# Where the resident slots are prepared at two changes of the resident set: one subtraction at the end of each quarter's list instead of up to two

## What is computed

```python
def ref(hidden_states, cross_attention_states, ...):   # 32 query heads, 8 key/value heads, width 128
    q = rmsnorm(hidden_states @ q_proj_w.T)            # per head
    k = rmsnorm(cross_attention_states @ k_proj_w.T)
    v = cross_attention_states @ v_proj_w.T
    attn = softmax(q @ k.T * scale + mask)
    return (attn @ v) @ o_proj_w.T

x = x + tanh(g_xattn) * ref(layernorm(x), ctx, ...)
x = x + tanh(g_ffn) * experts(layernorm(x), A, B, Wr)  # top 16 of 64 experts of rank 16, softmax gates
```

## Time and profile before

| | us |
|---|---|
| median of three runs | 2317.74 (2317.13 to 2318.9) |
| the profiled execution | 2318.4 |
| its span, first to last instruction | 2316.6 |
| TensorE busy | 2261.6 (98%) |
| VectorE busy | 1597.6 (69%) |
| ScalarE busy | 1183.9 (51%) |
| GpSimd busy | 1144.8 (49%) |
| mean granted clock of TensorE | 0.997 of full speed |

### The profile page before, as it was taken

How to read it: one execution, slowest core, us unless ns; L and a number is a source line. 1 busy time by engine, 2 the same in 40 slices (tenths; PEclk the granted TensorE clock), 3 DMA queues, 4 the chain that set the end, 5 groups by cost and what they waited for, 6 DMA issues and landing times.

```text
span 2316.6 us, 35630 instructions
## 1 busy us (share of the span) xinstructions
PE 2261.6 (98%) x11615; PEld 1906.0 (82%) x11615; DVE 1597.6 (69%) x2669; ACT 1183.9 (51%) x3773; POOL 1144.8 (49%) x1735
## 2 busy tenths in 40 slices
PE   6999999999999999999999999999999999999999
PEld 5887887888888878888888788888888887888787
DVE  7558558777777797777777954755756878555755
ACT  5546546666666676666666732422424335333421
POOL 3666566666555555555555453233232664534221
PEclk9999999999999999999999999999999999999999
DMA  5688466767667367764322635645557566323643
GB/s 198 218 245 296 150 197 232 212 165 204 183 170 191 121 212 205 230 179 128 110 91 92 209 100 164 182 127 166 162 152 216 186 217 255 128 92 136 237 164 136
DMA packets 177062, 408.78 MB, mean 176 GB/s; under 512 B 11824, under 2 KB 77616, under 8 KB 159664
## 3 DMA queue, kind: packets, MB, share of 16 engines
q1 hardware_dynamic: 169392, 351.97, 44.1%
q0 software_dynamic: 7488, 54.53, 12.9%
HBM read 282.72 MB, written 190.84 MB: 204 GB/s over the span
## 4 chain that ended last, share of the span: by engine, by line
PE 84%; DVE 4%; POOL 4%; issue 3%; ACT 3%; DMA 2%; SPq 0%; POOLq 0%; ACTq 0%; DVEq 0%
PE bank L769 23%; PE bank L771 23%; PE bank L770 23%; PE bank L827 4%; PE bank L835 2%; PE bank L815 2%; DVE t_lo L1320 1%; PE bank L852 1%; PE bank L851 1%; PE bank L850 1%; ACT t_hi L1024 1%; POOL s_hi L1811 1%; DVE s_lo L1320 1%; DMA t_raw<-combos 1%; DMA staged<-in_w_q 1%
## 5 line engine op out<-in xcount | busy, mean ns | idle before, releaser
L769 PE MATMUL bank<-t_hi,s_hi 128*128 128x512 f32 x2688 | 1084.0, 403 | 30.7 <-DVE t_lo L1320 17.3
L771 PE MATMUL bank<-t_hi,s_lo 128*128 128x512 f32 x2688 | 1053.8, 392 | 0.0
L770 PE MATMUL bank<-t_lo,s_hi 128*128 128x512 f32 x2688 | 1050.9, 391 | 0.0
L769 PEld LDWEIGHTS bank<-t_hi,s_hi 128*128 128x128 f32 x2688 | 507.2, 189 | 128.1 <-issue 32.3
L771 PEld LDWEIGHTS bank<-t_hi,s_lo 128*128 128x128 f32 x2688 | 505.8, 188 | 110.7
L1320 DVE TENSOR_TENSOR s_lo<-staged,s_hi 128x512 fp32r<-128x512 f32 x672 | 525.0, 826 | 88.9 <-ACT s_hi L1035 86.9
L770 PEld LDWEIGHTS bank<-t_lo,s_hi 128*128 128x128 f32 x2688 | 507.5, 189 | 90.3
L1035 ACT CAST s_hi<-staged 128x512 fp32r<-128x512 f32 x434 | 250.2, 623 | 184.9 <-POOL staged L1801 71.5
L1782 POOL TENSOR_SCALAR small<-small 128x4 f32<-128x4 f32 (+1 forms) x192 | 75.9, 395 | 446.9 <-ACT small L1131 341.4
L1799 POOL TENSOR_TENSOR staged<-staged 128x512 f32<-128x512 f32 x86 | 115.3, 1340 | 365.5 <-DMA staged<-heads 196.9
L1463 DVE SCALAR_TENSOR_TENSOR probs<-bank,small,mask 128x128 f32<-128x128 f32 x512 | 143.9, 343 | 87.1 <-POOL small L1789 43.6
(11 more groups left out here) (143 smaller groups left out, 2894.7 us busy)
## 6 DMA issues: line engine op xcount, KB each, us to landing
heads<-heads SPq DMA_DIRECT2D x128, 256.0 KB, 4.3
staged<-in_w_q SPq DMA_DIRECT2D x32, 768.0 KB, 5.2
staged<-heads SPq DMA_DIRECT2D x32, 768.0 KB, 6.9
sums<-sums POOLq DMA_DIRECT2D x24, 1024.0 KB, 8.0
t_raw<-in_sets SPq DMA_DIRECT2D x20, 1024.0 KB, 7.1
t_raw<-combos SPq DMA_DIRECT2D x19, 1024.0 KB, 8.6
xt<-x_columns SPq DMA_DIRECT2D x8, 1792.0 KB, 6.8
combos<-in_sets POOLq DMA_DIRECT2D x14, 1024.0 KB, 10.2
```

Source lines behind the costliest of these rows:

```text
L769: nc.tensor.matmul(out, s_hi[w][:, cols], high, start=start, stop=False, skip_group_check=True)
L770: nc.tensor.matmul(out, s_hi[w][:, cols], low, start=False, stop=False, skip_group_check=True)
L771: done = nc.tensor.matmul(out, s_lo[w][:, cols], high, start=False, stop=at == 3, skip_group_check=True)
```

## The change

It adds a third table of positions and uses it at the changes to sets 3 and 4 only.

```diff
+FILL_POSITIONS_QUERY = (2, 4, 6, 7, 9, 11, 11)
...
-            positions = FILL_POSITIONS_AHEAD if t in AHEAD_SETS else FILL_POSITIONS
+            positions = FILL_POSITIONS_QUERY if t in (3, 4) else FILL_POSITIONS_AHEAD if t in AHEAD_SETS else FILL_POSITIONS
```

## The result

| | before | changed |
|---|---|---|
| median of 7 runs, us | 2318.17 (2317.13 to 2319.04) | 2325.74 (2322.92 to 2327.12) |
| profiled execution, span | 2318.4, 2316.6 | 2324.77, 2323.0 |

The change makes the kernel slower: the ratio is 1.003 with a 95% interval of 1.0021 to 1.004, 7.6 us between the medians. The prediction said 2324.6, 6.9 above before.

The account below looks back on a forecast made before the run. TensorE, busy 98% of the span, was taken as the bound, with VectorE late at set changes. Waits of +4.1 and clock drops of +2.8 gave +6.9 us, 2324.6 on the median; range 2318.5 to 2329.5.

Parts of the forecast that it names:

- What bounds: At the two set changes VectorE is the late engine and TensorE waits; 6.7 and 6.8 us lost, 13.5 the prize.
- The first quarters give back: First two quarters of the new set shorten as VectorE's lists start earlier; 3.8 us in hand by the third.
- Slot 4: Third quarter of the new set: subtraction starts at 851.27, giving TensorE a new wait of 3.0 us.
- Slot 5: Third quarter's seventh part: subtraction usable at 861.0 to 861.8, a second new wait of 2.5 to 3.3, taken as 2.9.
- The clock: Half-clock drops behind the waits for slots 4 and 5: +1.4 us a change, +2.8 in all, bounds 0 and 6.6.
- the term for the waits alone: TensorE's waits at both set changes together, without any clock drop: +4.1 us.
- Totals: Both set changes: +4.1 us of waits and +2.8 of clock, +6.9 us in all.
- Rival 1: No clock drop at the set changes, the waits alone: +4.1 or +3.3, 2321 to 2322 us; chance 0.17.
- Rival 2: Two full clock drops at each set change, neither hidden: +10.7 us, 2328.4; chance 0.15.
- Rival 4: No difference: VectorE's lists run about 1 us shorter each change and the clock stays, within 3 us; chance 0.07.
- Rival 3: Faster: VectorE regains its ordinary distance before slot 4 is due, 7.6 us faster, 2310.1; chance 0.06.
- The rule on the oscillating clock: Skill's rule that waits make following work begin at half clock; all four long waits paid twice, +10.7 us.

Follow-up runs that it names:

- e6: Changed kernel with the four sums of staged formed for only 16 of 512 columns at the changes to sets 3 and 4: 2325.72 us, ratio 1.0032.
- e8: Kernel before with the four sums of staged formed for only 16 of 512 columns at the changes to sets 3 and 4: 2313.89 us, ratio 0.998.
- e2: Changed kernel with slots 4 and 5 each put back by one quarter: 2318.21 us, ratio 0.9995 to before.
- e3: Kernel before with slot 2 alone moved one quarter later, beside slot 3: 2318.91 us, ratio 1.0004.
- e9: Changed kernel with slot 4's and 5's subtractions ahead of the softmax in the same quarters, their ScalarE copies earlier: 2317.22 us, ratio 0.9996 to before.
- e5: Changed kernel with spare matmuls on TensorE, 10 ahead of slot 4's part and 8 ahead of slot 5's: 2324.19 us, ratio 1.0024 to before.
- e4: Kernel before with slots 5 and 6 alone moved to the third quarter of the new set's first quad: 2325.15 us, ratio 1.0025.
- e7: Changed kernel with slot 4's subtraction moved to GpSimd and slots 5 and 6 put back to the new set's second quarter: 2324.13 us, ratio 1.0027 to before.

## Why the prediction was right

**What bounds.** Right. The loss lies in the two stretches and the quarter behind each, and VectorE is full up to new r2 in nearly every version; in e6, with less work, it waits. e8 bears it out from the other side: with less VectorE work the kernel before gains 4.6 us, while none of the three other orders of the same work gained anything (e2, e3, e9 within their intervals). e8 also has `staged` ready earlier, and no run separates the two.

**The first quarters give back.** Right, and a little too small. Predicted starts of new r1 and r2, counted from new r0, were 8.15 and 17.55; they came at 7.92 and 16.90. The wait before L836 in new r0 was 0.40 and not 0.8, the one before L828 0.20 and not 0.8, and the second one before L836 1.01 against 1.25. The wait for s_lo went as said.

**Slot 4.** Right: subtraction predicted at 851.27, measured at 850.68; wait predicted at 3.0, measured at 2.77 and 3.01.

**Slot 5.** Right in place and cause: VectorE's own wait of 0.5 is there (0.55), the subtraction started at 858.95 (predicted 858.6 to 859.4) and was usable at 861.8 (861.0 to 861.8). The waits are 3.69 and 1.81 where I took 2.9 for both, with bounds of 2.5 and 3.3 that neither keeps. In the first change TensorE was at full clock and at the part earlier than I had it (858.12 against 858.47), and the subtraction lasted 2.76. In the second the clock had dropped behind slot 4, so that TensorE reached the part later: the half clock was hidden in this wait, as the section on the clock supposed. Slot 6 caused no wait in the changed kernel, as said.

**The clock.** About right as a sum as far as the runs tell, wrong in its parts. The drops came behind slot 5 in the first change (0.95 and 0.89 in the windows, 0.05 x 14.93 + 0.11 x 8.16 = 1.6 us) and behind slot 4 in the second (0.22 x 15.46 = 3.4 us, much of it inside the wait for slot 5). I had put one behind slot 4 in both. That the two changes came out alike is partly luck: with slot 5's wait at 3.69 in one and 1.81 in the other, the half clock changed places with the wait. e5 bears out about half of the 2.8 us: 1.6 less with one drop still there. Less that drop's 1.6 (8.91 - 7.33) e5 stands 5.7 - 1.6 = 4.1 above before, which is the term for the waits alone; one profile and two medians carry this, so I call it consistent and not shown.

**Totals.** Each change was to lose 3.5 us more than before. Up to new r3 the traces have 3.15 + 0.8 (new r3) and 3.79, more than I summed. The sum stopped there and put what follows at nothing; it gives back 0.8 and 0.6 (the two waits before L835 behind new r3 that are gone). Net it is 3.2 a change. The time came so near to the forecast, 7.6 against 6.9 between the medians, partly because these two errors are of opposite sign.

**The rivals.** Rival 1 (no drop) fell by the windows. Rival 2 (two drops a change) fell by the time, though single executions come near it: e6's profiled one has the two drops a change and took 2329.43, where rival 2 said 2328.4 for the changed kernel. Rival 4 fell. Rival 3 I had priced as unlikely for the right cause, that new r0's list is longer than TensorE's quarter, but its deciding point was put wrongly: "how far VectorE is behind in new r1" sounds as if less load would mend it. e6 took the load away and slot 4 came no earlier; e9 left the load and moved the two subtractions within their lists, with their copies ahead of them, and 8.5 us came back. So the price of the change is that slots 4 and 5 stand *behind the softmax of the quarter in which TensorE wants them*, slot 5 with its copy as well as its subtraction. Even then the time is only that of before; no version here that does all the work came near rival 3's 2310.

The rule on the oscillating clock (the Trainium skill, TensorE: Matmul & The Clock Gate, "HAM oscillation — how this bites in real kernels"), weighed in the prediction, would have each long wait paid twice. The page tells it of a loop with a DMA wait of about 3 to 5 us in every tile; here there are two single waits a change. In the changed kernel four long waits brought two stretches of half clock, not four, the second about twice as long as the first. In e6 all four waits (2.79 to 3.19) were followed by one, and e4's waits of 3.48 and 3.45 brought none (its windows of new r2 and r3 have 1.00; those of the first change stand below). So a single wait of this length may or may not bring half clock here: the rule held in e6's execution, half in the changed kernel's and not in e4's. No run shows what decides.

```profile
851.18:862.23 11.05, 7.57 (x45) 6.30 (x44) 10.78 (x18) 8.52 (x23) 8.21 (x9) 1.00 0.22 72
862.23:869.55 7.32, 7.32 (x44) 6.37 (x43) 5.96 (x8) 4.54 (x20) 6.99 (x11) 1.00 0.00 0
```

## What to carry to other kernels

When an engine is full over a whole stretch, look first for work to take out of it: here three other orders of the same work moved the stalls and removed none, and leaving work out did (e8). Before moving a piece later, ask not only in which list it stands but what stands ahead of it there and what that waits for: behind an instruction that follows the consumer, the piece is late by the consumer's own pace. At the head of the same quarter it cost nothing that could be measured here (e9). A wait that vanishes in front of an engine is a gain only if the deadline behind it still holds.

## What the runs showed of the hardware

VectorE and GpSimd hold each other up when both work in SBUF. GpSimd's scalar operations of 128x4 take 0.20 us; beside VectorE's subtraction (844.12, 2.28 us long, shown above) one of them took as long as the subtraction. In the changed kernel:

```profile
843.89 0.20 POOL L1786 TENSOR_TENSOR small<-small 128x4 f32<-128x4 f32 x1
844.17 2.28 POOL L1788 TENSOR_SCALAR small<-small 128x4 f32<-128x4 f32 x1
```

The other way, VectorE's norm took 3.07 instead of 0.69 in e7, and ended 0.55 behind GpSimd's subtraction. I had costed neither. The Trainium skill (SBUF — State Buffer, "SBUF: two separate sides") says that the two engines share a pair of ports which the instruction that begins first holds to its end, when VectorE has two SBUF inputs. Both rows agree with it in size: the late one ends 0.05 and 0.55 us behind the early one, no more than its own work of 0.20 and 0.69.
